# A two-block transformer kernel on one Trainium2 core: the projected cross values are kept in a full-width tile laid over the experts' second-layer weights, which are loaded in the sixteenth iteration

## What is computed

```python
h1 = adaln(x, t, norm1_w, norm1_b)
x = mha(h1, h1, attn1_wq, attn1_wk, attn1_wv, attn1_wo, attn1_bo) + x      # 16 heads of 64
h2 = adaln(x, t, norm2_w, norm2_b)
x = mha(h2, context, attn2_wq, attn2_wk, attn2_wv, attn2_wo, attn2_bo) + x # 16 heads, 77 keys
h3 = adaln(x, t, norm3_w, norm3_b)
x = glu_ff(h3, ff_w1, ff_b1, ff_w2, ff_b2) + x
```

## Time and profile before

| what | value |
|---|---|
| median of 3 runs | 979.17 us (976.92 to 979.4) |
| the profiled execution, its own time | 978.34 us |
| its span, first to last instruction | 976.5 us |
| mean granted TensorE clock | 0.895 of full speed |
| busy of the span: PE / DVE / ACT / POOL | 82% / 58% / 54% / 37% |
| DMA moved, mean rate | 88.53 MB, 91 GB/s |

### The profile page before, as it was taken

How to read it: one execution, slowest core, us unless ns; L and a number is a source line. 1 busy time by engine, 2 the same in 40 slices (tenths; PEclk the granted TensorE clock), 3 DMA queues, 4 the chain that set the end, 5 groups by cost and what they waited for, 6 DMA issues and landing times.

```text
span 976.5 us, 18039 instructions
## 1 busy us (share of the span) xinstructions
PE 801.4 (82%) x5701; PEld 655.0 (67%) x5701; DVE 568.3 (58%) x1941; ACT 526.2 (54%) x1139; POOL 359.6 (37%) x559
## 2 busy tenths in 40 slices
PE   6978898999996999789796669899996877762594
PEld 5756686777874787578575545799855666652493
DVE  2557785677863667477466453333367877886112
ACT  3555565667663665466365332233527888861362
POOL 1223443334331323233265415266621322224463
PEclk9999898999997999899898769999965879795697
DMA  8514304340700420120221013488450000000474
GB/s 269 171 52 146 126 14 144 115 156 23 249 1 27 144 75 1 44 53 10 61 75 44 11 44 115 120 249 250 142 184 0 1 1 1 1 1 27 141 205 133
DMA packets 82055, 88.53 MB, mean 91 GB/s; under 512 B 6155, under 2 KB 69851, under 8 KB 81323
## 3 DMA queue, kind: packets, MB, share of 16 engines
q1 hardware_dynamic: 78475, 80.19, 27.3%
q0 software_dynamic: 3488, 7.20, 2.1%
HBM read 69.03 MB, written 35.17 MB: 107 GB/s over the span
## 4 chain that ended last, share of the span: by engine, by line
PE 47%; DVE 19%; ACT 10%; issue 8%; DMA 7%; POOL 6%; SPq 3%; DVEq 0%; POOLq 0%; ACTq 0%
DMA v_all<-sb_v_rows 5%; PE bank L964 5%; PE bank L707 4%; PE bank L674 4%; PE bank L680 3%; DVE sb_smax L1472 3%; DVE sb_row_sum L1481 3%; PE bank L697 3%; PE bank L747 3%; PE bank L972 2%; PE bank L1073 2%; PE bank L1081 2%; DVE sb_st_all L1779 2%; PE bank L925 2%; POOL sb_expd L1956 2%
## 5 line engine op out<-in xcount | busy, mean ns | idle before, releaser
L1956 POOL TENSOR_TENSOR sb_expd<-sb_expd,sb_rden 128x512 f32<-128x512 f32 (+1 forms) x128 | 112.0, 877 | 290.1 <-DVE sb_rden L1485 290.0
L1472 DVE TENSOR_REDUCE sb_smax<-bank 128x4 f32<-128x512 f32 (+1 forms) x128 | 74.1, 579 | 69.5 <-PE bank L707 47.3
L2048 POOL TENSOR_TENSOR sb_rstd_all<-sb_rsq_all,sb_halves 128x4 f32<-128x4 f32 x44 | 45.2, 1026 | 133.2 <-DVE sb_rsq_all L1786 133.2
L1195 ACT ACTIVATE sb_expd<-sb_shifted 128x512 f32<-128x512 f32 (+1 forms) x128 | 69.6, 544 | 30.2 <-DVE sb_shifted L1475 28.7
L1481 DVE TENSOR_REDUCE sb_row_sum<-sb_expd 128x4 f32<-128x512 f32 (+1 forms) x128 | 73.0, 570 | 8.0 <-ACT sb_expd L1195 8.0
L1475 DVE TENSOR_TENSOR sb_shifted<-bank,sb_smax 128x512 f32<-128x512 f32 (+1 forms) x128 | 75.0, 586 | 4.4
L674 PE MATMUL bank<-sb_h1T,sb_watt 128*128 128x128 f32 x512 | 71.2, 285 | 4.7 <-DMA sb_watt<-att_w 2.4
L674 PEld LDWEIGHTS bank<-sb_h1T,sb_watt 128*128 128x128 f32 x512 | 63.1, 195 | 9.6 <-DVE sb_xb L1461 3.7
L964 PE MATMUL bank<-sb_blk_xT,sb_up_w 128*128 128x128 f32 x456 | 57.1, 275 | 0.0
L2014 POOL DMA_INDIRECT back_a<-sb_blk_y,sb_dest_a x38 | 37.0, 973 | 48.8 <-issue 25.8
L964 PEld LDWEIGHTS bank<-sb_blk_xT,sb_up_w 128*128 128x128 f32 x456 | 54.0, 192 | 0.0
(11 more groups left out here) (260 smaller groups left out, 2006.7 us busy)
## 6 DMA issues: line engine op xcount, KB each, us to landing
sb_up_w<-gate_up SPq DMA_DIRECT2D x38, 384.0 KB
sb_v<-v_all SPq DMA_DIRECT2D x16, 576.0 KB, 5.6
rows_b<-pad_b SPq DMA_DIRECT2D x7, 1105.0 KB, 10.1
rows_a<-pad_a SPq DMA_DIRECT2D x7, 975.0 KB, 8.4
sb_up_w<-w1b SPq DMA_DIRECT2D x23, 256.0 KB
v_all<-sb_v_rows SPq DMA_DIRECT2D x14, 308.0 KB
sb_blk_x<-rows_a SPq DMA_DIRECT2D x38, 65.0 KB, 3.3
sb_picked<-back_a SPq DMA_DIRECT2D x4, 512.0 KB, 5.5
```

Source lines behind the costliest of these rows:

```text
L1195: act.activation(exp_of(i, s, j), shifted[:, u % 2, :, 0:n], ACT.Exp, scale=DH ** -0.5).then_inc(exp_done, 1)
L1472: dve.tensor_reduce(smax[:, u % 2, :], s_in, X, ALU.max).then_inc(max_done, 1)
L1956: pool.tensor_tensor(e, e, rden[:, u % 2, :].unsqueeze(2).broadcast_to([P, QH, n]), ALU.mult).then_inc(norm_done, 1)
L2048: pool.tensor_tensor(rstd_all[:, c], rsq_all[:, 0, c], halves[:, c], ALU.pow).then_inc(root_ready[k], 1)
```

## The change

The tile `v2_rows` goes. In its place stands a view, 2048 columns wide, of the part of `moe_w` that `down` takes up later. A whole block fits, so the wait ahead of `v2_2` is taken out; the wait ahead of `v2_0` stays. The loads of `gate_up` and `down` move out of the start into SyncE's loop, to iteration 15 (the sixteenth from 0), behind the load of batch 14's values and a wait for all the stores. `tri` gets a semaphore of its own.

```diff
+        v2_rows = moe_w[:, 2 * CA * P:2 * CA * P + 2 * INNER]
...
-        v2_rows = sb1("v2_rows", P, INNER)
...
-        ld_vo2 = sem("ld_vo2")
+        ld_vo2, ld_tri = sem("ld_vo2"), sem("ld_tri")
...
-            sp.dma_start(gate_up[:, :], A["gate_up"][EA]).then_inc(ld_moe, 16)
-            sp.dma_start(down[:, :, :, :], A["down"]).then_inc(ld_moe, 16)
-            sp.dma_start(tri[:, :], A["tri"]).then_inc(ld_moe, 16)
+            sp.dma_start(tri[:, :], A["tri"]).then_inc(ld_tri, 16)
...
-                                     v2_rows[p0:p1, :].rearrange("p (h d) -> p h d", h=8)).then_inc(v2_stored, 16)
+                                     v2_rows[p0:p1, half * INNER:(half + 1) * INNER].rearrange("p (h d) -> p h d", h=8)).then_inc(v2_stored, 16)
...
+                if i == max(V2_BLOCK) + 1:
+
+                    sp.wait_ge(v2_stored, 16 * v2_stores(len(V2_BLOCK)))
+                    sp.dma_start(gate_up[:, :], A["gate_up"][EA]).then_inc(ld_moe, 16)
+                    sp.dma_start(down[:, :, :, :], A["down"]).then_inc(ld_moe, 16)
...
             def rank_sums(x, part, t):
 
                 pe.wait_ge(hot_ready[x], part + 1)
-                pe.wait_ge(ld_moe, 48)
+                pe.wait_ge(ld_tri, 16)
...
-            pe.wait_ge(ld_moe, 48)
+            pe.wait_ge(ld_moe, 32)
...
                     if name == "v2_0":
                         from_one(act, v2_stored, 16 * v2_stores(n))
-                    if name == "v2_2":
-                        act.wait_ge(v2_stored, 16 * (v2_stores(n) + len(v2_pieces(n))))
-                    empty(i, name, v2_rows[0:last, half % 2 * 512:(half % 2 + 1) * 512], lambda t: t[0:last, :])
+                    empty(i, name, v2_rows[0:last, half * 512:(half + 1) * 512], lambda t: t[0:last, :])
```

## The result

The median falls from 978.85 us (976.92 to 979.4, 4 runs) to 939.88 us (937.56 to 942.72, 4 runs): ratio 0.9607, 95% interval 0.9574 to 0.9639, 39.0 us (35.3 to 41.7). The forecast was 940.

What follows compares the result with a forecast made beforehand. ScalarE's ten DMA waits on the stores (50.1 us) and the slow TensorE clock behind them were taken as the bound. Savings of 30.7 + 4.0 + 4.5 = 39.2 us off 978.34 gave 939.1, forecast 940 us as median, range 933 to 952.

Steps and rivals of the forecast that it cites:

- The wait that goes: ScalarE's wait on the stores ahead of v2_2: removing it was to save 39.2 us in all.
- The floor: Length of a block's iteration without stall: 29.67 us, from i=14's 30.47 less 0.80 for slow clock.
- the terms for i=4 to 14: Savings of seven block iterations, each its length less 29.67 us, plus 0.8 us for i=12: 30.7 us.
- i=0 and 1: First two iterations: 4.5 us saved in i=0, nothing in i=1, where TensorE's wait for VectorE remains.
- a slow pair of L680: TensorE's two L680 groups behind a stall in i=0 and i=3, taken as about half their time at full clock.
- The wait that stays: Wait ahead of v2_0 for the block before, worst from iteration 8 to 9: no wait, 5 us margin.
- rival (a): Part of the wait comes back at v2_0 of i=9 and the load for i=10: 953 us, chance 0.13.
- SyncE's queue: Load of values behind iteration 8's stores, needed in i=10: 12 us left, cost 0, up to 3 us in range.
- The moved loads: gate_up and down between the loads of batch 14 and 15: latter some 10 us later, over 30 us cover, no cost.
- Rival (d): Late weights make the last cross_out wait on batch 15's load, kernel slower: over 982 us, chance 0.02.
- Rival (b): A block's extra fills hide in TensorE's gaps: gain up to 50 us, time 929 us, chance 0.06.
- Rival (c): No gain, because ScalarE's stand hid behind something else all along: 979 us, chance 0.03.

Runs made afterwards that it cites:

- e1: Kernel before with only the loads moved and tri's own semaphore, narrow tile and v2_2 wait kept: 994.4 us against 994.4, ratio 1.000.
- e2: Changed kernel with only ScalarE's wait ahead of v2_2 put back: 991.94 us against 994.4 for the kernel before, ratio 0.9991.
- e4: Changed kernel run once more, no edit: 954.93 us against 994.4 for the kernel before, ratio 0.9608.
- e3: Kernel before with each store piece cut into a multiple of 16 rows and a rest: 966.64 us against 994.4, ratio 0.9732.
- e7: Changed kernel with gate_up and down loaded only after the first phase: 948.46 us against 978.61 for the kernel before, ratio 0.9704.
- e6: Changed kernel with block 5 stored a second time, to an unread DRAM tensor: 960.8 us against 978.61 for the kernel before, ratio 0.9832.
- e9: Changed kernel with the wait ahead of v2_2 put back in iteration 8 alone: 963.07 us against 994.13 for the kernel before, ratio 0.9693.
- e5: Changed kernel with each store piece cut into a multiple of 16 rows and a rest: 940.88 us against 978.61 for the kernel before, ratio 0.9620.

## Why the prediction was right, step by step

**The wait that goes.** Right in kind (e1 and e2 leave nothing over) and in size. The floor, 29.67 us from the one iteration whose stall hid in TensorE's work, came out at 29.2 to 29.6; the terms for i=4 to 14, 30.7 us by the prediction, measured 32.5, since the floor was 0.2 us too high on average. i=3: 4.0 forecast, 4.1 measured. i=0 and 1: 4.5 forecast, 4.6 by the means of the profiles, though from the pair before and after alone one would have read 1.8. The split was less good than the sum: 4.5 and nothing forecast, 3.8 and 0.8 read. One working was loose: a slow pair of L680 was taken at double its time at full clock, which would make a pair 0.84 us; at full clock it takes 1.02 (the first row of e4). Together 39.2 forecast and 41.2 by these readings; the medians say 39.0, with 35.3 to 41.7 as their interval. That forecast and median agree to 0.2 us is luck; that they agree to 3 us is not.

**Where the profiled pair differs from the sum.** The spans differ by 35.6 us, and the iterations 3 to 14 alone give 36.6. Less than forecast came from i=0 and 1 (1.8 us of the 4.5); taken back are 0.8 us before the first scores and 2.1 us from i=15 to the end of the phase. The first two are chance between executions (first scores between 20.4 and 22.4 us in all runs, i=0 and 1 between 60.8 and 64.5 us in the changed kernel). The last is too, as far as the runs go: the stretch takes 67.5 us in e2, which has the moved load, and 69.7 and 70.3 us in e3 and e7, which have it not. In the rows the lost time is slow clock. The stretch before and after, and `cross_out` in i=16 before, which takes 4.33 us after:

```profile
506.24:574.16 67.92, 45.77 (x295) 37.92 (x294) 34.47 (x101) 25.76 (x46) 30.16 (x47) 0.80 0.13 37
```

```profile
468.38:538.42 70.04, 48.29 (x295) 40.56 (x294) 34.66 (x101) 25.77 (x46) 30.16 (x47) 0.78 0.19 64
```

```profile
537.25 3.65 PE L697 MATMUL bank<-sb_v,sb_probT 128*128 128x128 f32 x20
```

The same 295 matmuls keep TensorE busy 2.5 us longer, and its idle time is 0.4 us shorter. Why the low clock fell on that stretch in one run and not in another was not tried. What follows the first phase takes 402.4 us before and 402.5 after, unchanged as forecast.

**The wait that stays.** The worst case was named rightly, and its size: stores through at 310.22, `v2_0` at 315.53, 5.3 us of margin against 5 forecast. e6 shows that the wait is real: stores that took 22.1 us longer, less the 5.3 us of margin, made the 16.7 us of wait. This was rival (a)'s mechanism, and it is absent only by those 5 us. It rests on the serial halves, which e6 shows (four halves, 45 us) and the profile after as well, by a stretch of its first half and one of its second:

```profile
288.00:294.00 6.00, 6.00 (x33) 3.59 (x34) 2.33 (x11) 3.79 (x9) 2.65 (x6) 1.00 0.07 21
298.00:304.00 6.00, 5.83 (x58) 5.42 (x58) 4.51 (x13) 3.38 (x7) 2.64 (x3) 1.00 0.08 23
```

Each is about one engine's work of 16, not two at once. Whether it is the same engine in both, as it would be by the rule of the Trainium skill (DMA: Bandwidth & Descriptors, section "Why a DMA increments its semaphore by 16 and not by 1"), was not shown.

**SyncE's queue.** The load after block 5 was issued at 310.22, i=10 began at 322.83, and no wait of TensorE for `sb_v<-v_all` is in the view of waits: 12.6 us, 12 forecast.

**The moved loads.** `down` landed 8.9 us after its issue, at 481.7, over 70 us before its first reader. Batch 15's load was to come 10 us later. It was issued right behind `down`, at 473.30, 4.9 us into the iteration where it had been 4.3; what grew was its time to landing (up to 9.7 us, against 5.3 before). It was there 36 us ahead of the last `cross_out` (519.69). The price without cover is 7 to 8 us (e7). Rival (d) would have needed far more than the load can cost anywhere.

**Rival (b)**, the fills hidden in TensorE's gaps: the iterations with a block lie 1.1 to 1.5 us over i=7, not at it. A part does hide: TensorE is busy 28.97 us in i=6 and 25.81 in i=7, 3.2 us more, for 1.4 us of time; the floor read from i=14 had that in it already.

**Rival (c)** falls with e2.

## What to carry to other kernels

A stall's price is not the wait that the profile shows. Take the iteration length against a floor, from a like iteration whose stall is small and whose bounding engine is busy throughout; here 50 us of waits were worth 39, while the longest of them alone, 10.5 us, was worth 11.1 (e9): a short stall hides in part in the run-ahead, and behind a long one the slow clock eats what the run-ahead saves. Count the slow clock of TensorE that a stall leaves behind too: 0.9 us in i=12 and 1.3 in i=9, the next iteration alone.

Where a buffer is too small, look for a tile whose contents are needed late: its load can be moved if it has cover at the new place, and its price without cover is about the load's time from issue to landing (6.9 us here for 1.9 MB; the kernel lost 7 to 8).

Before making room, look at why the transfer is slow. Cutting the pieces at multiples of 16 rows gave about two thirds of the gain without any new space, though one iteration's wait grew by it.

## What the runs showed of the hardware

- A store of 53 rows of 8 x 512 bytes runs at 22 GB/s, with a DMA share of 0.07 of 16 engines, and the piece of 75 rows issued behind it moves only at the end: two pieces, 0.5 MB, 12 us. With 48 + 5 and 64 + 11 rows the wait for the same bytes was 2.27 us in the place of 10.49.
- SyncE is held too: the issue behind the slow piece took 8.1 us, a later one up to 10.1, and the four issues of i=8 together 16.7 us before and 19.2 after; cut evenly, eight took 3.8.
- A stall of 16.7 us cost 17.8 in its iteration, though TensorE had work to run ahead with: the mean granted clock of that window was 0.82, against 1.00.
- In the changed kernel two chips gave iterations 3 to 14 the same length to 0.05 us, and the rest of the program after the first phase 13 us apart (402.4 us in e5, 415.5 in e4).
